# Forty edge buckets with halved sources, ranks summed on TensorE, and basis loads in 2 KB pieces

## The chip, the cores and the metric

The kernel runs on one core of one Trainium2 chip. The metric is the device time of one execution in microseconds; lower is better. Three executions of the kernel before took 2352.77 to 2354.81 us, median 2353.74.

## What is computed

```python
h = relu(layernorm(x))                       # x: 1250 nodes x 512
x = x + L0(h, edges, noise)                  # 4 blocks, each:
    # y = cond_layer_norm(x); q, k, v = y@wq, y@wk, y@wv, 4 heads of 128
    # scores only along 20000 edges src -> dst, softmax per src node, sum of v[dst]
    # x += attention @ wo;  x += relu(cond_layer_norm(x) @ m_w1) @ m_w2
h = relu(layernorm(x))
x = x + L1(h, edges, edge_type)              # 2 relational layers, each:
    # w[r]  = sum_b att[r, b] * basis[b]     # r in 0..1, b in 0..29, basis[b]: 512 x 512
    # gate  = sigmoid(x @ gate_w[r]);  msg[r] = (gate * x) @ w[r]
    # out   = sum over edges of type r of msg[r][dst] -> src,  + x @ root + bias
```

Edges may repeat, so both parts need, for each pair of nodes, how many edges of each type lie between them. The kernel makes this count matrix (1250 x 1250 x 2) on the chip and uses it as a bias of the scores (the logarithm of the count) and as the matrix of the relational sums. The combined relational weights w[r] take all 60 basis matrices, 1 MB each, through the chip.

## The kernel before, in words

Each of the five engines runs its own program in order, and semaphores tie them. The first 320 us hold three things at once.

**Edges to counts.** 20,000 edges lie as 128 x 157 in SBUF. DVE gives each edge a bucket (10 tiles of 125 destination nodes x 2 types, NB = 20), makes `mask[128, NB, EC]`, its running sum `cum` (L1641), and from the totals per bucket (two small matmuls, L824 and L825) the place of each edge in an order by bucket in which each bucket is padded to whole groups of 256 edges (L1648 to L1661). Then 10 sort batches (L1674 to L1682) build one-hot matrices on DVE, and PE (L841) moves source and destination numbers to their places. Then NG = 98 groups are counted: DVE builds `src_hot[128, 2, 1254]` (one-hot over all source nodes, L1705) and `dst_hot` (L1702), PE multiplies them into 3 banks of PSUM (6 matmuls of 418 columns, L859), ACT copies the result to 16-bit integers (`count_add`, L1328), and DVE adds it to the bucket's slice of `count` (L1716). There are two buffers of `src_hot` and of `count_add`; the addition of a group comes one iteration (two groups) behind its one-hots.

**Basis to relational weights.** SP loads the basis matrices in 80 loads of 768 KB (`load_bases`, L549), each 96 partitions (16 rows x 6 bases) x 8 KB, into a ring of 6 buffers; the ring frees a buffer when PE has used it. PE contracts each with the attention coefficients (`relation_loads`, 4 matmuls, L812). ACT stores the 16 results to HBM (L1278, L1280). PE takes its loads at fixed places of its program: 5 ahead of the sort, 2 or 3 behind each sort batch, and one behind every second count group (LOADS_FIRST, LOADS_SORT, LOADS_COUNT). Ahead of load 11 SP waits for ACT's `node_relu` (L1269) and stores x; ahead of load 65 it queues weights of the first block.

**Preparation** of the noise embedding (DVE L1619 to L1623, ACT L1284 to L1300, POOL L759), the normalisation of x (ACT), and constants on POOL (L701 to L721). POOL clears `count` (L773) when the places are known.

Then ten tiles of score biases are made and stored together with the counts (`adj`), and the four blocks run until about 1,950 us. Each relational layer then makes messages for ten tiles and sums them: for each tile t PE needs the counts of the tile, which SP loads (`load_adj`, L528) two tiles ahead into two buffers, and ACT turns to fp32 (`adj_hi`, L1536). Between the layers SP also loads the second layer's weights (`load_r`, L519, 8 transfers of 64 partitions for each type), queued ahead of the counts:

```python
sp.wait_ge(r_mm_ps, 3 * NT * (l + 1))
if l == 0:
    for n in range(3):
        load_r(1, n)
for t in range(NT):
    n = NT * l + t
    if n + 2 < 2 * NT:
        sp.wait_ge(r_adj_lo, n + 1)
        load_adj(n + 2)
```

## Time and profile before

| | us |
|---|---|
| median of three runs | 2353.74 (2352.77 to 2354.81) |
| profiled execution, its own time | 2352.55 |
| its span | 2350.8 |
| PE busy | 2202.4 (94%) |
| DVE busy | 1593.8 (68%) |
| ACT busy | 1119.3 (48%) |
| POOL busy | 546.2 (23%) |
| DMA moved | 189.56 MB |

The page's 40 slices are each 58.8 us long. The DMA row reads 9 8 9 9 9 6 in the first six, and 0 to 4 nearly everywhere behind; DVE's reads 9 9 8 9 9 8 there. PE's row is at 9 from the fifth slice on, with two exceptions in the slices 6 and 8, and at 2 and 8 in the first two. So the stretch up to about 320 us has other limits than the rest.

### The profile page before, as it was taken

Reading aid. Unit: us, or ns where it says so; the run is one execution under the profiler, and the core shown is the slowest. Engines: PE = TensorE matmul, PEld = TensorE weight load, DVE = VectorE, ACT = ScalarE, POOL = GpSimd, SP = SyncE. Lnnn points to the kernel's source line nnn. Section 1 sums busy time; section 2 is a strip of 40 time slices with the busy share of each in tenths; the row PEclk is TensorE's granted clock in tenths of the full one; section 3 lists DMA queues with packets and bytes.
Section 4 is the critical chain, followed back from the end, with each engine's and each line's share of the span. In section 5 each row is a group of like instructions: output and inputs, shape, how many; then the busy total and the mean of one; then the engine's idle time right before and its main releaser. Section 6 shows DMA issues by size and latency. Waiting matters only on the chain.

```text
span 2350.8 us, 36257 instructions
## 1 busy us (share of the span) xinstructions
PE 2202.4 (94%) x13797; PEld 1899.8 (81%) x13797; DVE 1593.8 (68%) x3322; ACT 1119.3 (48%) x1806; POOL 546.2 (23%) x401
## 2 busy tenths in 40 slices
PE   2889968999999999999999999999999999999998
PEld 1456647899988889988888998898899888877887
DVE  9989986478776458877646887763787774244233
ACT  5146652377743347763335775233677533222321
POOL 6000000066510026650003663000566200000000
PEclk9899978999999999999999999999999999999999
DMA  9899963111031011003102003111110421062034
GB/s 253 220 250 253 274 203 123 44 31 44 1 113 66 21 52 44 22 37 101 52 20 65 22 23 98 64 37 31 44 44 1 134 73 29 17 103 43 1 69 105
DMA packets 110945, 189.56 MB, mean 81 GB/s; under 512 B 57893, under 2 KB 58341, under 8 KB 103099
## 3 DMA queue, kind: packets, MB, share of 16 engines
q1 hardware_dynamic: 106776, 180.47, 28.9%
q10 hardware_dynamic: 4003, 6.79, 1.1%
q8 instruction: 114, 1.87, 0.3%
q14 instruction: 52, 0.43, 0.1%
HBM read 155.16 MB, written 32.07 MB: 80 GB/s over the span
## 4 chain that ended last, share of the span: by engine, by line
PE 75%; DVE 11%; issue 5%; ACT 5%; DMA 2%; DVEq 1%; SPq 1%; POOL 0%; ACTq 0%; POOLq 0%
PE PS L1043 10%; PE PS L1071 9%; PE PS L962 6%; PE PS L964 6%; PE PS L963 6%; PE PS L1057 6%; PE PS L948 5%; PE PS L952 4%; PE PS L949 4%; PE PS L1199 4%; PE PS L1209 4%; PE PS L859 3%; PE PS L812 2%; ACT prob L1433 1%; DMA basis_t<-in_L_gnn_basis_dram 1%
## 5 line engine op out<-in xcount | busy, mean ns | idle before, releaser
L793 POOL TENSOR_SCALAR prob<-prob,inv_den 125x1000 f32<-125x1000 f32 x160 | 444.5, 2778 | 0.0
L781 POOL TENSOR_TENSOR rstd<-var_eps,neg_half 125x2 f32<-125x2 f32 x45 | 35.4, 787 | 907.1 <-DVE var_eps L1596 907.1
L1433 ACT ACTIVATE prob<-prob,neg_max 125x1254 f32<-125x1254 f32 x160 | 215.5, 1347 | 56.9 <-DVE neg_max L1936 56.7
L1931 DVE CUSTOM_DVE_ANT_0 prob<-PS,sbias 125x1254 f32<-125x1254 f32 x160 | 233.0, 1456 | 11.0 <-issue 8.4
L1071 PE MATMUL PS<-pT_hi,v_hi 125*128 125x250 f32 x800 | 236.0, 295 | 0.0
L1950 DVE TENSOR_TENSOR pT_lo<-PS,pT_hi 125x1000 fp32r<-125x1000 f32 x160 | 191.1, 1194 | 51.2 <-ACT pT_hi L1450 51.2
L1071 PE MATMUL PS<-pT_lo,v_hi 125*128 125x250 f32 x800 | 224.1, 280 | 0.0
L1071 PE MATMUL PS<-pT_hi,v_lo 125*128 125x250 f32 x800 | 222.3, 278 | 0.0
L1057 PE MATMUL PS<-ident,prob 125*125 125x125 f32 x1600 | 201.7, 273 | 5.6 <-DVE pT_lo L1953 5.5
L1057 PEld LDWEIGHTS PS<-ident,prob 125*125 125x125 f32 x1600 | 196.1, 189 | 12.6 <-issue 7.6
L1448 ACT ACTIVATE pT_hi<-PS 125x1000 fp32r<-125x1000 f32 x160 | 161.8, 1011 | 82.7 <-PE PS L1057 82.7
L1328 ACT ACTIVATE count_add<-PS 125x1254 int16<-125x1254 f32 x98 | 118.9, 1215 | 72.3 <-PE PS L859 66.9
L1071 PEld LDWEIGHTS PS<-pT_lo,v_hi 125*128 125x128 f32 x800 | 151.9, 190 | 0.2
L1043 PE MATMUL PS<-k_hi,q_hi 128*125 128x418 f32 x480 | 125.0, 368 | 28.7 <-DVE row_max L1931 23.5
L1071 PEld LDWEIGHTS PS<-pT_hi,v_hi 125*128 125x128 f32 x800 | 151.6, 190 | 0.2
L1071 PEld LDWEIGHTS PS<-pT_hi,v_lo 125*128 125x128 f32 x800 | 151.3, 189 | 0.0
L859 PEld LDWEIGHTS PS<-src_hot,dst_hot 128*125 128x125 bf16 x588 | 100.7, 196 | 58.1 <-DVE src_hot L1705 54.4
L859 PE MATMUL PS<-src_hot,dst_hot 128*125 128x418 bf16 x588 | 132.4, 362 | 0.4 <-DVE src_hot L1705 0.4
L1510 ACT ACTIVATE hT_lo_raw<-PS,cols_all 128x250 f32<-128x250 f32 x80 | 37.5, 469 | 192.3 <-PE PS L952 192.3
L792 POOL TENSOR_TENSOR pool_slot<-pool_slot 1x1 f32<-1x1 f32 x160 | 29.3, 183 | 427.6 <-DVE inv_den L1944 427.6
L2102 DVE TENSOR_TENSOR adj_lo<-adj,adj_hi 125x2500 fp32r<-125x2500 int16 x20 | 55.2, 2762 | 99.2 <-PE PS L1209 87.1
L1043 PE MATMUL PS<-k_lo,q_hi 128*125 128x418 f32 x480 | 118.2, 355 | 0.0
(330 smaller groups left out, 5628.2 us busy)
## 6 DMA issues: line engine op xcount, KB each, us to landing
basis_t<-in_L_gnn_basis_dram SPq DMA_DIRECT2D x80, 768.0 KB, 12.5
sbias<-score_bias SPq DMA_DIRECT2D x40, 548.6 KB
adj<-adj SPq DMA_DIRECT2D x20, 546.9 KB
w_lo_raw<-in_L_gnn_m_w_dram SPq DMA_DIRECT2D x8, 1024.0 KB, 6.5
score_bias<-biases SPq DMA_DIRECT2D x10, 548.6 KB
adj<-count SPq DMA_DIRECT2D x10, 546.9 KB
xc<-x_lat SPq DMA_DIRECT2D x12, 448.0 KB
x_first<-x_lat SPq DMA_DIRECT2D x10, 448.0 KB
```

What stands on the lines that cost most here:

```text
L793: pool.tensor_scalar(prob[u % 3][:, 0:SPLIT], prob[u % 3][:, 0:SPLIT], inv_den[0:T, u % 4:u % 4 + 1], None, ALU.mult)\
L859: g = pe.matmul(PS[0:T, 3 * b + j, 0:SB], dst_hot[n // 2 % 2][:, 0:T, 2 * b + h], src_hot[b][:, h, SB * j:SB * (j + 1)], start=(h == 0), s ...
L962: pe.matmul(o, x_hi[:, k, n], w_hi[:, k, :], start=(k == 0), stop=False)
L963: pe.matmul(o, x_hi[:, k, n], w_lo[:, k, :], start=False, stop=False)
L964: g = pe.matmul(o, x_lo[:, k, n], w_hi[:, k, :], start=False, stop=(row3 is None and k == 3))
L1043: g = pe.matmul(PS[0:T, j, 0:SB], q_t[:, h, n], k_t[:, h, SB * j:SB * (j + 1)], start=(x == 0), stop=(x == 2))
L1057: g = pe.transpose(PS[0:T, 3 + k // 4, T * (k % 4):T * (k % 4 + 1)], prob[u % 3][:, T * k:T * (k + 1)], ident[0:T, 0:T])
L1071: g = pe.matmul(PS[:, 6 + s, 0:W], v_t[:, k, f], p_t[:, k, :], start=(k == 0 and x == 0), stop=(k == NT - 1 and x == 2))
L1433: act.activation(prob[u % 3][:], prob[u % 3][:], ACT.Exp, bias=neg_max[0:T, u % 4:u % 4 + 1], accum_out=den[0:T, u % 4:u % 4 + 1]).then_in ...
L1448: act.activation(pT_hi[i % 2][:, 0:8, n].rearrange("p (b c) t -> p b c t", b=2), PS[0:T, 3:5, 0:4 * T].rearrange("p b (c t) -> p b c t", c ...
L1931: v.tensor_tensor_reduce(prob[u % 3][:].rearrange("p (j s) -> p j s", j=3), PS[0:T, 0:3, 0:SB], sbias[p % 2][a][:].rearrange("p (j s) -> p ...
L1950: v.tensor_tensor(pT_lo[i % 2][:, 0:8, n].rearrange("p (b c) t -> p b c t", b=2), PS[0:T, 3:5, 0:4 * T].rearrange("p b (c t) -> p b c t", ...
```

## The change

1. NK = 40 buckets (NB = 20 before): type x destination tile x half of the sources. `count` is [125, 40, 628] in place of [125, 20, 1254], groups are NG = 118 in place of 98 (TC = 236 columns of places in place of 196), and a group has 4 matmuls of 314 columns in place of 6 of 418. `src_hot` and `count_add` have four buffers, and the addition comes two iterations behind.
2. Ranks: `mask` and `cum` are 16-bit and twice as long (6,280). The sum over buckets that DVE did in fp32 (L1655 to L1657) is split in a low part (DVE, 40 `tensor_scalar` and 4 products) and a high part (ACT, 40 activations), and PE adds the 40 slices of each with an identity matrix (80 matmuls of 157 columns). The table from groups to buckets is made by a transpose and one matmul. POOL makes a table `bucket_no[128, 40, 157]` ahead of `chunk_no`, `slot_no` and `group_no`, and DVE waits for all of them (14 constants).
3. Each basis load is four transfers of 96 partitions x 2 KB; the rows of a result follow. `load_r` therefore has 32 transfers of 16 partitions for each type in place of 8 of 64. PE takes 3 loads behind each sort batch and 3 behind every 8 count groups (79 ahead of the bias stage, as before).
4. In the relational layers `load_adj` comes ahead of `load_r`, and the three `load_r` are spread over the tiles 0 to 2.
5. `adj` is stored from the halves, in rows of 1,250 bytes (2,500 before).

```diff
-    NG = (EC * 128 + NB * (GE - 1)) // GE
+    NH = N // 2
+    HW = 628
+    HP = HW // 2
+    NK = 2 * NB
+    NG = (EC * 128 + NK * (GE - 1)) // GE
...
-        src_hot = [m(f"src_hot{i}", [128, 2, SW], bf16) for i in range(2)]
+        src_hot = [m(f"src_hot{i}", [128, 2, HW], bf16) for i in range(4)]
...
-        LOADS_SORT = [2 + b % 2 for b in range(SORT_BATCHES)]
-        LOADS_COUNT = [n % 2 for n in range(NG)]
+        LOADS_SORT = [3] * SORT_BATCHES
+        LOADS_COUNT = [3 * (n + 1) // 8 - 3 * n // 8 for n in range(NG)]
...
                     for k in range(D // GR):
-                        p0 = GR * (k % 2)
-                        sp.dma_start(wr_raw[n][p0:p0 + GR, k // 2, :],
-                                     rel_w[l, k, :, :].rearrange("(j r i) d -> r i j d", j=4, r=R)[n]).then_inc(rel_in[n], 16)
+                        for j in range(4):
+                            p0 = GR * (k % 2) + GROUP_I * j
+                            at = GROUP_I * (R * j + n)
+                            sp.dma_start(wr_raw[n][p0:p0 + GROUP_I, k // 2, :], rel_w[l, k, at:at + GROUP_I, :]).then_inc(rel_in[n], 16)
...
-                sp.dma_start(basis_t[n % RING][:], rows.rearrange("b (i j) d -> i b (j d)", j=4)).then_inc(basis_in[n % RING], 16)
+                for j in range(4):
+                    sp.dma_start(basis_t[n % RING][:, j, :], rows[:, GROUP_I * j:GROUP_I * (j + 1), :].rearrange("b i d -> i b d"))\
+                        .then_inc(basis_in[n % RING], 16)
...
                 sp.wait_ge(r_mm_ps, 3 * NT * (l + 1))
-                if l == 0:
-                    for n in range(3):
-                        load_r(1, n)
                 for t in range(NT):
                     n = NT * l + t
                     if n + 2 < 2 * NT:
                         sp.wait_ge(r_adj_lo, n + 1)
                         load_adj(n + 2)
+                    if n < 3:
+                        load_r(1, n)
...
+            pool.iota(bucket_no[:], [[1, NK], [0, EC]], base=0, channel_multiplier=0,
+                      allow_small_or_imprecise_dtypes=True).then_inc(consts, 1)
...
+            pe.wait_ge(rank_step, BASES)
+            for part in range(4):
+                pe.wait_ge(rank_step, LOW_RANKS + part)
+                for k in range(NK // 4 * part, NK // 4 * (part + 1)):
+                    pe.matmul(PS[:, 5, 0:EC], ident16[:], cum[:, k, :], start=(k == 0), stop=(k == NK - 1))
+            for part in range(4):
+                pe.wait_ge(rank_hi_done, part + 1)
+                for k in range(NK // 4 * part, NK // 4 * (part + 1)):
+                    g = pe.matmul(PS[:, 4, 0:EC], ident16[:], rank_hi[:, k, :], start=(k == 0), stop=(k == NK - 1))
+            g.then_inc(rank_ps, 1)
...
-            link(v.tensor_tensor(rank[:], cum[:], base[:].unsqueeze(2).to_broadcast([128, NB, EC]), ALU.add))
-            link(v.tensor_tensor(rank[:], rank[:], mask[:], ALU.mult))
-            link(v.tensor_reduce(pos[:], rank[:].rearrange("p k c -> p c k"), AX.X, ALU.add))
...
+            link(v.scalar_tensor_tensor(base_lo[:], base_hi[:], -128.0, base[:], ALU.mult, ALU.add))
+            for part in range(4):
+                ks = slice(NK // 4 * part, NK // 4 * (part + 1))
+                for k in range(ks.start, ks.stop):
+                    last = v.tensor_scalar(cum[:, k, :], cum[:, k, :], base_lo[:, k:k + 1], None, ALU.add)
+                link(last)
+                v.tensor_tensor(cum[:, ks, :], cum[:, ks, :], mask[:, ks, :], ALU.mult).then_inc(rank_step, 1)
+            v.wait_ge(rank_ps, RANK_PS)
```

On DVE, the ranks, from the running sum to the first one-hot of the sort. Before:

```order
L1641 SCALAR_TENSOR_TENSOR cum<-mask 128x3140 [waits chain]
...
L1655 TENSOR_TENSOR rank<-cum,base 128x3140 [waits chain]
L1656 TENSOR_TENSOR rank<-rank,mask 128x3140 [waits chain]
L1657 TENSOR_REDUCE pos<-rank 128x157 [waits chain]
L1658 TENSOR_SCALAR pos_c<-pos 128x157 [waits chain]
```

In the change (the middle two parts of four are like the first):

```order
L1680 SCALAR_TENSOR_TENSOR cum<-mask 128x6280 [waits chain]
...
L1704 TENSOR_SCALAR cum<-cum,base_lo 128x157 [waits chain]
L1704 TENSOR_SCALAR cum<-cum,base_lo 128x157 x9
L1706 TENSOR_TENSOR cum<-cum,mask 128x1570 [waits chain]
...
L1708 TENSOR_SCALAR pos<-PS 128x157 [waits rank_ps]
```

DVE now waits for PE between the last product and the places.

On SP, from the first relational layer's messages to its sums. Before:

```order
L519 DMA wk_lo_raw<-rel_w 64x1x512 [waits r_mm_ps]
L519 DMA wk_lo_raw<-rel_w 64x1x512 x7
L519 DMA wv_lo_raw<-rel_w 64x1x512 x8
L515 DMA wq_lo_raw<-in_L_gnn_root_dram 128x4x512
L528 DMA adj_136<-adj 112x20x125 [waits r_adj_lo]
L528 DMA adj_136<-adj 13x20x125
```

In the change:

```order
L542 DMA adj_136<-adj 112x20x125 [waits r_adj_lo,r_mm_ps]
L542 DMA adj_136<-adj 13x20x125
L534 DMA wk_lo_raw<-rel_w 16x512 x32
L542 DMA adj_137<-adj 112x20x125 [waits r_adj_lo]
L542 DMA adj_137<-adj 13x20x125
L534 DMA wv_lo_raw<-rel_w 16x512 x32
L542 DMA adj_136<-adj 112x20x125 [waits r_adj_lo]
```

The counts of tile 2 stand first, and 32 transfers stand between two loads of counts.

## Rows read from the trace of the kernel before

**Rows 1.** Windows of four stretches (busy us per engine, PEclk, DMA share, GB/s).

```profile
core 0: us, PE busy (x) PEld busy (x) DVE busy (x) ACT busy (x) POOL busy (x), PEclk, DMA share, GB/s
140.00:235.00 95.00, 94.83 (x530) 58.28 (x526) 94.39 (x184) 66.64 (x60) 0.00 (x0) 1.00 1.01 253
300.00:310.00 10.00, 10.00 (x57) 6.00 (x57) 10.00 (x21) 7.78 (x7) 0.00 (x0) 1.00 0.12 41
651.00:654.00 3.00, 2.86 (x25) 2.66 (x24) 1.51 (x2) 3.00 (x6) 2.92 (x2) 1.00 1.04 399
673.00:678.00 5.00, 5.00 (x28) 4.10 (x27) 3.96 (x10) 1.99 (x3) 0.70 (x1) 1.00 1.08 235
```

**Rows 2.** DMA issues by line (KB each, median us to landing).

```profile
basis_t<-in_L_gnn_basis_dram SPq DMA_DIRECT2D x80, 768.0 KB, 12.5
```

**Rows 3.** Chain that ended last, 30 to 135 us (start, us, what).

```profile
115.92 17.18 DMA basis_t<-in_L_gnn_basis_dram
```

**Rows 4.** Groups of instructions, 135 to 312 us (busy, mean ns | idle before).

```profile
L859 PE MATMUL PS<-src_hot,dst_hot 128*125 128x418 bf16 x588 | 132.4, 362 | 0.4 <-DVE src_hot L1705 0.4
L1328 ACT ACTIVATE count_add<-PS 125x1254 int16<-125x1254 f32 x97 | 117.7, 1215 | 72.2 <-PE PS L859 66.9
L1705 DVE TENSOR_SCALAR src_hot<-node_no,slot_src 128x1254 bf16<-128x1254 f16 x192 | 95.3, 535 | 0.0
L1716 DVE TENSOR_TENSOR count<-count,count_add 125x1254 int16 x96 | 76.4, 796 | 0.5 <-issue 0.3 <-ACT count_add L1328 0.2
L1702 DVE TENSOR_TENSOR dst_hot<-slot_no,slot_dst 128x512 bf16<-128x512 f16 x48 | 19.6, 409 | 5.3 <-PE PS L859 5.2
```

**Rows 5.** Timeline of all engines, 311 to 357 us (start, us, line, what).

```profile
313.66 0.81 DVE L1716 TENSOR_TENSOR count<-count,count_add 125x1254 int16 x1 [0.52 <-ACT count_add L1328]
```

**Rows 6.** Timeline of DVE, 0 to 62 us.

```profile
14.57 3.43 DVE L1638 TENSOR_TENSOR mask<-bucket,bucket_id 128x3140 bf16<-128x3140 f32 x1
...
18.03 6.70 DVE L1641 TENSOR_TENSOR_SCAN cum<-mask 128x3140 f32<-128x3140 bf16 x1
...
27.09 3.43 DVE L1655 TENSOR_TENSOR rank<-cum,base 128x3140 f32<-128x3140 f32 x1
...
34.02 5.83 DVE L1657 TENSOR_REDUCE pos<-rank 128x157 f32<-128x3140 f32 x1
...
41.17 2.95 DVE L1674 TENSOR_SCALAR chunk_hot<-chunk_no,pos_c 128x196 f16<-128x196 f16 x16
...
44.05 1.21 DVE L1678 TENSOR_TENSOR place_hot<-edge,slot_no 128x2048 f16<-128x2048 f16 x1
```

**Rows 7.** Timeline of POOL, 0 to 100 us.

```profile
2.53 2.47 POOL L717 IOTA slot_no<- 128x2048 f16 x1
...
15.06 10.51 POOL L730 TENSOR_TENSOR att_z<-att_rows,row_of 96x80 f32<-96x80 f32 x4 [7.46 <-DMA att_rows<-in_L_gnn_att_dram]
...
47.88 10.57 POOL L773 MEMSET count<- 125x12540 f32 x1
```

**Rows 8.** Line L1674, 49 to 62 us (ns min/median/max).

```profile
L1674 DVE TENSOR_SCALAR chunk_hot<-chunk_no,pos_c x16: 253/258/8440, 50.1 to 60.8; 128x196 f16<-128x196 f16 x16
```

**Rows 9.** Timeline of PE, 0 to 140 us.

```profile
32.90 6.30 PE L812 MATMUL PS<-basis_t,att_z 96*32 96x512 f32 x40
```

**Rows 10.** Costliest groups of the page.

```profile
L1510 ACT ACTIVATE hT_lo_raw<-PS,cols_all 128x250 f32<-128x250 f32 x80 | 37.5, 469 | 192.3 <-PE PS L952 192.3
```

**Rows 11.** Timelines of SP, ACT and PE, 2,040 to 2,280 us.

```profile
2050.49 5.74 SPq L519 DMA_DIRECT2D wk_lo_raw<-rel_w  x8
...
2056.26 5.05 SPq L519 DMA_DIRECT2D wv_lo_raw<-rel_w  x8
...
2276.15 0.33 SPq L686 DMA_DIRECT2D xres<-x_lat  x1
...
2072.12 2.29 ACT L1536 ACTIVATE adj_hi<-adj 125x2500 fp32r<-125x2500 int16 x1 [21.03 <-DMA adj<-adj]
...
2074.46 5.93 PE L1199 MATMUL PS<-msg_hi,adj_hi 125*125 125x512 f32 x18 [5.35 <-ACT adj_hi L1536]
```

More of the change, by code:

```diff
@@ L1289, in _ @@
             act.activation(cols_all[:, 2:4, :], cols[:, 2:4, :], ACT.Copy).then_inc(cols_out, 1)
+            act.wait_ge(rank_step, BASES)
+            for k in range(NK):
+                h = act.activation(rank_hi[:, k, :], mask[:, k, :], ACT.Copy, scale=base_hi[:, k:k + 1])
+                if (k + 1) % (NK // 4) == 0:
+                    h.then_inc(rank_hi_done, 1)
             act.wait_ge(z1_ps, 1)
```

196 lines of the change are left out of this document (110 added, 86 removed).

## The prediction

> **What bounds the kernel now.** I read the page's 40 slices first: DMA is busy in nine tenths only at the beginning, PE in nine tenths only behind it. So I cut the first 320 us into windows. From 140 to 235 us the DMA share is 1.01 at 253 GB/s, and DVE is busy in 94.39 of 95 us; by 300 to 310 us the share is down to 0.12 while counting goes on [rows 1]. Two limits lie side by side there: the 80 basis transfers of 768 KB, 786 KB in thousands of bytes [rows 2], which at 253 GB/s take 3.1 us each, and the vector work of 98 groups. The chain of waits shows what ends last in the sort: it runs over two long waits for a basis load, the second of them 17.18 us [rows 3]. In the counting the groups of instructions tell the rest: DVE was idle 5.3 us ahead of `dst_hot` and hardly elsewhere, while ACT waited 66.9 us for PE's groups [rows 4]. So the sort is held by the basis and the counting by DVE; the last addition ends at 313.66 + 0.81 = 314.5 us [rows 5]. All that follows waits for it, and PE is then the bound to the end. What the change does ahead of 314.5 us therefore counts in full, once.
>
> **The change, part by part.**
>
> *Start of the sort.* The order on DVE is unchanged up to the bucket, but DVE now waits for 14 constants, among them `bucket_no`. POOL's `slot_no` took 2.47 us for 2,048 elements [rows 7], 1.21 ns each, so 6,280 take 7.6 us more ahead of the mask. The mask is two times 3,140 elements, but 16-bit on its input too: at the 1.21 us of `place_hot` for 2,048 [rows 6] it takes 3.7 against 3.43. The scan took 6.70 us for 3,140 [rows 6] with 16-bit input already, so 13.4: +6.7. The ranks cost DVE two products of 3.43 and a sum of 5.83, 12.7 us in all [rows 6]; now 40 short operations, at the 0.18 us of a `chunk_hot` (2.95 / 16, [rows 6]) 7.2 us, and four products of 1,570 elements, by `place_hot` 0.93 each: 10.9 us, -1.8. Behind them stands the wait on PE, which is new. PE is to finish five basis loads first; they began at 32.90 and took 6.30 us [rows 9], and they wait for `att_z`, which POOL begins at 15.06 and makes for 10.51 us [rows 7]. With the constants 7.6 us later and a longer DVE lock (POOL's 10.51 us already hold gaps for DVE) they end at 48 to 52. ACT's 40 activations of 157 columns, at 469 ns for 250 fp32 columns [rows 10], are 12 us at about 0.3 each, parallel to DVE; PE's last 40 sums follow part by part. That gives about +7 us. Sum: 7.6 + 6.7 - 1.8 + 7 + 2.5 for the short steps around them = 22 us: the sort starts at about 63.5 instead of 41.2. The bounds: +14 if PE and ACT keep up wholly, +30 if POOL and DVE lock each other out more. One such lock is in the trace: an operation of 258 ns took 8440 ns [rows 8], until POOL's clearing of `count` (47.88 + 10.57, [rows 7]) was over; it stays.
>
> *Vector work of sort and counting.* In the sort DVE makes 16 `chunk_hot` of 236 columns instead of 196 (about 0.19 us) and three products of 1.21 to 1.5 per batch: 6.6 to 7 us, ten batches and the lock, 76 us. Alone it would end at 63.5 + 76 + 8 for the two first batches and PE's tail, near 148. In the counting a group cost 2 x 535 + 796 + 409 / 2 = 2,070 ns by [rows 4], but (314.5 - 133.1) / 98 = 1.85 us by the clock, since neighbouring operations overlap (133.1 is where the counting begins, 115.92 + 17.18 [rows 3]). Half as wide, `src_hot` is about 0.3 us and the addition 0.41; `dst_hot` stays at 0.205 per group. 0.59 + 0.41 + 0.205 = 1.2, by the same overlap 1.15 to 1.17. 118 groups: 138 us in place of 181. ACT's copy, 1,215 ns for 1,254 columns [rows 4], comes to 0.65 to 0.76 for 628; PE's four matmuls of 314 to 0.66, and three loads per eight groups add 0.4. Neither reaches 1.17. So DVE alone would be ready at 148 + 138 + 2 = 288 us: **26 us earlier**.
>
> *The basis stream.* It must keep up, and this is the unknown. Its limit is a rate. Load 12 waits for ACT's `node_relu` and the stores of x, which move with the start by 21 us, to about 85 us. From there 68 loads follow: in the kernel before 64 + 68 x (3.11 + 0.2) + 10 = 299 us (0.2 for the stores of results, 10 for the weights of the first block and gaps), which fits the quiet DMA at 300 us [rows 1]. After: 85 + 68 x (786 / rate + 0.2) + 10. What is the rate of 96 partitions x 2 KB? No transfer of the trace has that shape. Weights of 128 partitions x 2 KB came at 399 GB/s, x in 112 partitions x 2 KB at 235 [rows 1], the basis in 96 x 8 KB at 253. Of the two slow shapes one is no whole number of quarters of the partitions, the other has long pieces; the new one has neither fault, and in pieces it is nearest to the 399. But it reaches three quarters of the partitions, so three quarters of 399, 299 GB/s, is what I hold for the ceiling. The bounds are 235 and 299, beyond them 399 only if partitions don't matter. I take 290, a little under the ceiling, because the stream also pays SP's time: a piece of `load_r` took SP 5.05 / 8 to 5.74 / 8 us, a row of x in 125 pieces of 2 KB 0.33 [rows 11], so four pieces cost 1.3 to 2.9 us beside the 2.7 us of the transfer. Then the last load ahead of the bias is there at 85 + 68 x 2.91 + 10 = 293, DVE's path gives 288, and with both near the end the counting ends at **294 us, -20.5**.
>
> [...]
>
> *Relational layers.* SP queued 17 transfers of `load_r` ahead of the counts of tile 2, the first at 2050.49; ACT, idle for 21.03 us, had the counts only at 2072.12, and PE stood 5.35 us [rows 11]. Now the counts go first, and this wait goes: -5.4. What is late next: 32 transfers of 16 partitions stand between two counts. At 0.63 us each as above they take SP 20 us, at the 0.33 of `xres` [rows 11] 11 us; PE needs some 10 us for a tile (two halves, the first of which took 5.93 us for most of its matmuls, [rows 11]). At 0.33 each count is queued about when PE begins the tile two ahead of its own, and nothing stalls. At 0.63 the counts of tile 4 are queued at 2050 + 2 x 21.5 = 2093, used at 2100 instead of 2088, and PE stalls 12 us there: +12 - 5.4 = +7. Sixteen pieces are fewer than either row has, so I take 0.33 to 0.4 and put back 2 us: net **-3.4**, with -5.4 and +7 as bounds.
>
> *Small edits.* `adj` in rows of 1,250 bytes: twice the pieces for 5.5 MB, beside the bias stage, which waits for other things; +1.5 (0 to 3). `load_r` of the last blocks in four times the pieces, hidden by PE's work of many us; +0.5. The transpose for `group_tile` is on PE in the sort: nothing, the cover is DVE's batch.
>
> **Sum**: -20.5 - 3.4 + 1.5 + 0.5 = -21.9 us. The profiled execution took 2352.55, 1.2 under the median, so 2330.6 for it, and 2332 against the median of 2353.74.
>
> **Rivals.**
>
> *The rate stays at 253.* A partition still gets the same 8 KB, and the early loads of the x tiles show that 2 KB alone doesn't make a transfer fast (235). Then 85 + 68 x 3.31 + 10 = 320, DMA ends the counting at about 319: +4.5 - 1.4, time **2357**. For it: the bytes per partition and the partitions are the same. [...] The point from which the change pays is (314.5 - 85 - 10) / 68 - 0.2 = 3.03 us a load, 260 GB/s.
>
> *In between*, 262 to 282 GB/s: the counting ends between 311 and 298, time **2335 to 2350**; also where SP's issue of 2.9 us a load becomes the limit, or where the 32 transfers between the counts of the relational layer stall PE.
>
> *Small transfers are slower: 235 GB/s, the rate of the 112 x 2 KB row.* 85 + 68 x 3.54 + 10 = 336, in the sort and counting some 333: +18.5 - 1.4, **2371**, slower than before. For it: that row is the only 2-KB one with part of the partitions. Against it: those transfers had small ones of 13 partitions between them.
>
> *A fully quick stream* (over 320): DVE's 288, time 2326; with `bucket_no` and PE's wait cheaper than I put them, 2320.
>
> **Numbers.** My forecast, 290 to 320 and more, has 0.40 (2320 to 2334); in between 0.18; the rate stays 0.26; lower 0.16. A measurement of this kernel tells 0.2%, 4.7 us, from no change. Faster: 0.40 + 0.16 of the second = 0.56. The same: 0.02 + 0.16 of the third = 0.18. Slower: 0.10 of the third, where the sort starts later than I put it, + 0.16 = 0.26. The range from 2319 to 2366 leaves out 0.05 below and half of the last rival above.
>
> **What would show it.** `bucket_no` on POOL at 7.6 us, the scan at 13.4, the first `chunk_hot` at about 63 (of a range of 55 to 71). In windows of the stretch from 100 to 280 us: GB/s near 290 and a DMA share under 1 at times. The groups: `src_hot` near 300 ns, the addition at 410, 1.17 us a group. The last addition near 294. In the first relational layer no wait of PE on `adj_hi` at tile 2. I am wrong if DMA is at a share of 1.0 with 253 GB/s or less and DVE waits for PE in the counting, if the sort begins after 71 us, or if a new wait of over 5 us stands at the tiles 3 to 5.

## The result and the profile after

| | before | after |
|---|---|---|
| median, us | 2353.26 (2350.09 to 2354.81, 4 runs) | 2384.11 (2383.26 to 2385.77, 4 runs) |
| ratio | | 1.0139, interval 1.0125 to 1.0153 |
| span of the profiled execution | 2350.8 | 2381.5 |

The change makes the kernel 31 us slower; 2332 with a range from 2319 to 2366 was forecast. I laid both traces side by side and read off when each stage begins. `csum` is DVE's first operation behind the last addition, `bias_mod` its first one of block 0 behind the score biases.

| stage begins, us | before | after | behind by | lost in the stage before it |
|---|---|---|---|---|
| sort (first `chunk_hot`) | 41.2 | 57.2 | 16.0 | 16.0 |
| counting (first matmul) | 135.0 | 150.3 | 15.3 | -0.7 |
| score biases (first `csum`) | 314.6 | 323.6 | 9.0 | **-6.3** |
| block 0 (`bias_mod`) | 355.2 | 370.5 | 15.3 | **+6.3** |
| x of the relational part (`xr`) | 1904.1 | 1925.2 | 21.1 | **+5.8** |
| end | 2350.8 | 2381.5 | 30.7 | **+9.7** |

So there are four places. The first three rows are the part on which the forecast stood: there the counting was to win 43 us and won 6. The column before is one execution, and two of its stages move. In the runs below that leave them as they are, `csum` began up to 3.5 us earlier (f and m), and the stage from `xr` to the end took 449 to 453 us instead of 446.7 (b, c, l and m). So the change lost 9 to 12.5 us ahead of `csum`, and 3 to 10 us in the last stage.

**The basis stream** did what was hoped, and more. Windows of the changed kernel (columns as in [rows 1]):

```profile
core 0: us, PE busy (x) PEld busy (x) DVE busy (x) ACT busy (x) POOL busy (x), PEclk, DMA share, GB/s
120.00:180.00 60.00, 53.72 (x374) 30.24 (x372) 46.37 (x119) 22.42 (x35) 2.84 (x1) 0.94 1.06 310
200.00:240.00 40.00, 31.45 (x190) 17.17 (x189) 34.40 (x96) 20.21 (x30) 0.00 (x0) 1.00 0.67 211
340.00:370.00 30.00, 13.44 (x60) 11.93 (x60) 20.82 (x18) 9.22 (x13) 0.00 (x0) 0.61 1.05 295
```

310 GB/s over 60 us, where the kernel before had 253 [rows 1]; from 200 us on the share is 0.67: the transfers wait for PE (SP 13.4 us in the 40, PE for no load), no longer the other way round. The last window is in the bias stage, and comes up below.

**Start of the sort.** Timeline of POOL, then of DVE, in the changed kernel:

```profile
3.88 6.01 POOL L775 IOTA bucket_no<- 128x6280 f16 x1
```

```profile
19.64 3.45 DVE L1678 TENSOR_TENSOR mask<-bucket,bucket_no 128x6280 f16<-128x6280 f16 x1
23.12 13.24 DVE L1680 TENSOR_TENSOR_SCAN cum<-mask 128x6280 f16<-128x6280 f16 x1
...
55.07 0.32 DVE L1708 TENSOR_SCALAR pos<-PS 128x157 f32<-128x157 f32 x1 [4.30 <-PE PS L863]
...
57.19 3.14 DVE L1728 TENSOR_SCALAR chunk_hot<-chunk_no,pos_c 128x236 f16<-128x236 f16 x16
...
62.63 3.85 DVE L1736 TENSOR_TENSOR dst_place<-place_hot,edge 128x2048 f16<-128x2048 f16 x1
66.40 12.34 DVE L1728 TENSOR_SCALAR chunk_hot<-chunk_no,pos_c 128x236 f16<-128x236 f16 x16
```

`bucket_no` took 6.01 us and the scan 13.24, twice that of [rows 6]; DVE waited 4.30 us for PE's sums. The last two rows show DVE held by POOL in the first two batches, as in [rows 8]: POOL's `z * z` ran from 61.97 for 3.42 us and its clearing of `count` from 65.34 for 10.58.

**The counting.** Groups of instructions of the changed kernel from 152 to 322 us (busy, mean ns | idle before), the counterparts of [rows 4]:

```profile
L892 PE MATMUL PS<-src_hot,dst_hot 128*125 128x314 bf16 x464 | 94.1, 325 | 34.5 <-DVE src_hot L1757 33.8 <-ACT count_add L1366 0.7
L1366 ACT ACTIVATE count_add<-PS 125x628 int16<-125x628 f32 x117 | 81.1, 694 | 83.7 <-PE PS L892 78.9 <-DVE count L1768 4.7
L1757 DVE TENSOR_SCALAR src_hot<-node_no,slot_src 128x628 bf16<-128x628 f16 x228 | 76.4, 378 | 0.0
...
L1768 DVE TENSOR_TENSOR count<-count,count_add 125x628 int16 x116 | 56.4, 486 | 23.9 <-issue 17.3 <-ACT count_add L1366 2.6 <-DVE count L1768 0.9
```

PE now stands 34.5 us, ACT 83.7; DVE stands 23.9 us ahead of its additions, 17.3 of it with the releaser "issue". That word means that nothing the profile shows kept it. Two groups in DVE's timeline show the pattern:

```profile
205.25 0.42 DVE L1754 TENSOR_TENSOR dst_hot<-slot_no,slot_dst 128x512 bf16<-128x512 f16 x1
205.58 0.67 DVE L1757 TENSOR_SCALAR src_hot<-node_no,slot_src 128x628 bf16<-128x628 f16 x2
206.37 0.49 DVE L1768 TENSOR_TENSOR count<-count,count_add 125x628 int16 x1
206.77 0.67 DVE L1757 TENSOR_SCALAR src_hot<-node_no,slot_src 128x628 bf16<-128x628 f16 x2
207.62 0.49 DVE L1768 TENSOR_TENSOR count<-count,count_add 125x628 int16 x1 [0.18 <-issue]
208.15 0.43 DVE L1754 TENSOR_TENSOR dst_hot<-slot_no,slot_dst 128x512 bf16<-128x512 f16 x1
```

From 205.25 to 208.15 a pair of groups takes 2.90 us, 1.45 a group (and (323.6 - 150.3) / 118 = 1.47 over all). The operations of one group need no more than 0.59 + 0.39 + 0.17 = 1.15 from start to start if they follow closely. The rest is between them: ahead of an addition 0.2 us, and 0.53 from the last addition to `dst_hot` where 0.40 would do. The run without reads, below, takes just these 1.15 us.

What the engine's sequencer does in these gaps is not counted as busy, but the view of one source line lists it. First the line that reads the table in the changed kernel, then the one in the kernel before (ns min/median/max):

```profile
L1763 DVEq FUSED_REGOPS  x230: 53/190/216, 152.3 to 322.6; - x115
L1763 DVEq TENSOR_LOAD <-group_tile x118: 298/304/1117, 151.7 to 322.2; - x118
```

```profile
L1711 DVEq TENSOR_LOAD <-group_tile x98: 299/305/1105, 137.4 to 312.4; - x98
```

Each group has one `TENSOR_LOAD` of 0.30 us, one register operation of 0.19 behind it and short steps around them. They are as long before as after; what changed is the work beside which they run.

**Last block and relational layer.** SP's timeline, PE's, and from the table of waits DVE's wait for x (engine, line, what ended it: us in total, times, longest):

```profile
1867.74 15.86 SPq L534 DMA_DIRECT2D wk_lo_raw<-rel_w  x32
1883.64 2.62 SPq L524 DMA_DIRECT2D xc<-x_lat  x6
...
2076.86 16.44 SPq L534 DMA_DIRECT2D wk_lo_raw<-rel_w  x32
2093.34 2.37 SPq L542 DMA_DIRECT2D adj<-adj  x2
...
2111.99 2.41 SPq L542 DMA_DIRECT2D adj<-adj  x2
```

```profile
2102.76 6.35 PE L1232 MATMUL PS<-msg_hi,adj_hi 125*125 125x512 f32 x20 [3.23 <-ACT adj_hi L1574]
...
2121.60 7.10 PE L1232 MATMUL PS<-msg_hi,adj_hi 125*125 125x512 f32 x20 [7.85 <-ACT adj_hi L1574]
```

```profile
DVE xc L2035 <- DMA xc<-x_lat: 3.0, 1, 3.0
```

32 transfers of 16 partitions occupy SP for about 16 us, 0.5 us each, where 8 of 64 partitions took 5 [rows 11]. In the last block the loads of x stand behind them, in the relational layer the counts of tiles 3 and 4: PE stands 3.23 and 7.85 us, in place of the 5.35 on tile 2 [rows 11], which is gone. And a stall costs more than its length: the 20 matmuls behind it took 6.35 and 7.10 us instead of 4.8. Behind the second stall the granted clock was 0.50 from 2,121 to 2,126 us; the mean from 2,100 to 2,120 is 0.82. The 5.35 us of before [rows 11] had the same sequel, 6.39 us for the 20 matmuls.

### The profile page after: what moved, and what is told of

Its sections match the earlier page's. It is cut to its first block, busy times and chain, and to the rows that moved or that the text cites. A ratio compares the mean times of both kernels' runs of the same rounds, so it can differ in the third digit from the quotient of the medians.

```text
span 2381.5 us, 36959 instructions
## 1 busy us (share of the span) xinstructions
PE 2183.4 (92%) x13763; PEld 1884.0 (79%) x13763; DVE 1577.8 (66%) x3441; ACT 1095.4 (46%) x1866; POOL 551.7 (23%) x403
## 4 chain that ended last, share of the span: by engine, by line
PE 71%; DVE 11%; issue 6%; ACT 5%; SPq 3%; DVEq 2%; DMA 2%; POOL 0%; ACTq 0%
PE PS L1076 10%; PE PS L1104 9%; PE PS L995 6%; PE PS L997 6%; PE PS L996 6%; PE PS L1090 6%; PE PS L981 5%; PE PS L985 4%; PE PS L982 4%; PE PS L1232 3%; PE PS L1242 3%; SPq L534 2%; ACT prob L1471 1%; DVE src_hot L1757 1%; PE PS L916 1%
## 5 line engine op out<-in xcount | busy, mean ns | idle before, releaser
L892 PEld LDWEIGHTS PS<-src_hot,dst_hot 128*125 128x125 bf16 x472 | 68.0, 197 | 88.6 <-DVE src_hot L1757 85.0
L809 POOL TENSOR_TENSOR pool_slot<-pool_slot 1x1 f32<-1x1 f32 x160 | 29.5, 185 | 427.6 <-DVE inv_den L1996 427.6
L892 PE MATMUL PS<-src_hot,dst_hot 128*125 128x314 bf16 x472 | 95.5, 324 | 34.5 <-DVE src_hot L1757 33.8
L1366 ACT ACTIVATE count_add<-PS 125x628 int16<-125x628 f32 x118 | 81.7, 694 | 92.4 <-PE PS L892 87.6
```

Source lines behind the costliest of these rows:

```text
L892: g = pe.matmul(PS[0:T, 2 * b + j, 0:HP], dst_hot[n // 2 % 2][:, 0:T, 2 * b + h], src_hot[n % 4][:, h, HP * j:HP * (j + 1)], start=(h == 0 ...
```

## The experiments

All times are medians, each beside runs of the kernel before on the same chip; the ratio to it is given with its 95% interval. Subtractions of two variants mostly go across chips, on which the kernel before has medians from 2350.3 to 2353.3, so differences of under 3 us say nothing. One reading has to be made with care: in the profiles of the runs f and m, whose work ahead of it takes as long as that of before, `csum` began at 311.2 and 311.0 instead of 314.6, so a difference of 3 us ahead of it proves nothing.

### One read of the table less in each group (run d)

```diff
-                k = v.value_load(group_tile[0:1, bass.ds(2 * it + b, 1)], min_val=0, max_val=NK - 1)
-                tile = count[:, bass.ds(k, 1), :].rearrange("p a s -> p (a s)")
+                tile = count[:, 20 * b, :]
```

> The changed kernel, with the addition always going to bucket 0 or 20 in place of the one read from the table of groups (so the counts are not the edges'). Theory: in short groups DVE's sequencer is the limit, with the reading of the table's number the costliest step; DVE is idle 0.18 to 0.26 us ahead of each addition (issue). Without it a group takes 1.25 us instead of 1.46: 25 us less, 2359. Rival: the group is bound by DVE's operations themselves (0.67 + 0.49 + 0.21 us) and the wait on PE and ACT; then 1.4 us or more and at least 2377.

Measured: 2344.38 us, ratio 0.9978 (0.9966 to 0.9989), 40 us under the changed kernel. The timeline of DVE:

```profile
202.23 0.41 DVE L1754 TENSOR_TENSOR dst_hot<-slot_no,slot_dst 128x512 bf16<-128x512 f16 x1
202.57 0.66 DVE L1757 TENSOR_SCALAR src_hot<-node_no,slot_src 128x628 bf16<-128x628 f16 x2
203.16 0.47 DVE L1767 TENSOR_TENSOR count<-count,count_add 125x628 int16<-125x628 int16 x1
203.55 0.66 DVE L1757 TENSOR_SCALAR src_hot<-node_no,slot_src 128x628 bf16<-128x628 f16 x2
204.14 0.47 DVE L1767 TENSOR_TENSOR count<-count,count_add 125x628 int16<-125x628 int16 x1
204.53 0.41 DVE L1754 TENSOR_TENSOR dst_hot<-slot_no,slot_dst 128x512 bf16<-128x512 f16 x1
```

A pair takes 2.30 us, 1.15 a group, without a gap; `csum` begins at 287.6. The operations are as long as ever (0.66 and 0.47). So the operations had been priced well in the forecast, and the read was missing from it. Of the 40 us, 36.5 lie in the counting (136.8 us from its first matmul to `csum` instead of 173.3), 0.31 us a group, where I had expected 0.21; 4.4 lie in the bias stage. The edit also makes the address of the addition a fixed one, so this run alone doesn't part the read from what follows it; the next but one does.

### The same reads, placed ahead (run i)

```diff
+                    ks = [read_group(it - 2, b) for b in range(2)]
                     for b in range(2):
                         one_hot(it, b, turn)
-                        add_group(it - 2, b, turn)
+                        add_group(it - 2, b, turn, k=ks[b])
```

> The changed kernel, with the two numbers of a pair of groups read from the table ahead of the pair's one-hots instead of each just ahead of its addition (as many reads as before). Theory A: a read costs DVE's sequencer its own time (0.31 us a group, by the run without reads), wherever it stands; then a group still takes 1.46 us and the time is 2384 within 4. Theory B: what costs is the latency between the read and the addition that uses it; then it hides behind the one-hots, a group takes 1.2 us and the time is near 2355.

Measured: 2410.42 us, ratio 1.0253 (1.0238 to 1.0267), worse than either theory had it. DVE's timeline:

```profile
204.18 0.67 DVE L1757 TENSOR_SCALAR src_hot<-node_no,slot_src 128x628 bf16<-128x628 f16 x2
204.77 0.48 DVE L1772 TENSOR_TENSOR count<-count,count_add 125x628 int16 x1
206.43 0.42 DVE L1754 TENSOR_TENSOR dst_hot<-slot_no,slot_dst 128x512 bf16<-128x512 f16 x1 [1.18 <-PE PS L892]
```

Nothing stands ahead of an addition any more, but 1.18 to 1.43 us stand ahead of `dst_hot`, once in a pair. The profile writes this wait to PE (the semaphore that came last in the row's wait), but PE's last group ahead of it was over at 204.91 + 0.81 = 205.72, 0.71 us before `dst_hot` starts. What lies there till the end is the two reads. PE's row, and the line of the reads on DVE's sequencer from 204.8 to 206.3 us (ns min/median/max, first and last start):

```profile
204.91 0.81 PE L892 MATMUL PS<-src_hot,dst_hot 128*125 128x314 bf16 x4 [0.17 <-DVE src_hot L1757]
```

```profile
L1762 DVEq FUSED_REGOPS  x3: 57/190/190, 205.2 to 205.9; - x3
L1762 DVEq TENSOR_LOAD <-group_tile x2: 299/300/301, 204.9 to 205.6; - x2
L1762 DVEq SEQ_ASSERT  x2: 23/23/23, 205.5 to 206.2; - x2
```

The first `TENSOR_LOAD` starts at 204.9, 0.1 us behind the start of the addition, the second at 205.6, and the last step of the reads at 206.2, 0.2 us ahead of `dst_hot`. PE then stood 1.78 us for the next `src_hot`, until 207.50. The pair takes 3.57 us, 1.27 more than without reads. Theory B is out: it isn't latency that could be hidden by reading early. Theory A is out in its second half, "wherever it stands": the earlier place lost what cover the reads had.

### Each read twice (run j)

```diff
-                k = v.value_load(group_tile[0:1, bass.ds(2 * it + b, 1)], min_val=0, max_val=NK - 1)
+                for _ in range(2):
+                    k = v.value_load(group_tile[0:1, bass.ds(2 * it + b, 1)], min_val=0, max_val=NK - 1)
```

> The changed kernel with each number read twice from the table, one read behind the other. Theory A (sequencer time, nothing hides it): another 0.31 us or a little less for each of 118 groups, 2384 + 30 to 37 = 2414 to 2421. If the first read's cost is one of waiting for the operations ahead of it, the second is nearly free and the time is under 2395.

Measured: 2460.76 us (2 executions), ratio 1.0466 (1.0448 to 1.0484); over the changed kernel 76.65 us, and 76.65 / 118 = **0.65 us a read**. That is twice what I expected. All of it is in the counting, which takes 249.9 us instead of 173.3. Only reads were added here, so it is the read. The first read of a group costs 0.31 (the run without reads), the second 0.65. DVE's timeline, and the line of the reads on its sequencer from 203.7 to 205.2 us, show one group:

```profile
203.73 0.67 DVE L1757 TENSOR_SCALAR src_hot<-node_no,slot_src 128x628 bf16<-128x628 f16 x2
205.28 0.48 DVE L1769 TENSOR_TENSOR count<-count,count_add 125x628 int16 x1 [0.89 <-issue]
```

```profile
L1764 DVEq FUSED_REGOPS  x3: 75/190/190, 203.7 to 204.7; - x3
L1764 DVEq TENSOR_LOAD <-group_tile x2: 304/304/305, 203.8 to 204.4; - x2
L1764 DVEq SEQ_ASSERT  x2: 23/23/23, 204.3 to 205.0; - x2
```

The first read starts at 203.8 and runs while DVE works on the `src_hot` pair, until 204.40; the second starts at 204.4 and finds nothing left to run beside, and DVE stands 0.89 us ahead of the addition. The reads ahead fit as well: 1.27 us more in a pair are 0.64 for each of its two reads. The `TENSOR_LOAD` has only 0.30 of the 0.65 us.

### No reads in the kernel before (run m)

```diff
-                k = v.value_load(group_tile[0:1, bass.ds(2 * it + b, 1)], min_val=0, max_val=NB - 1)
-                tile = count[:, bass.ds(k, 1), :].rearrange("p a s -> p (a s)")
+                tile = count[:, 10 * b, :]
```

> The kernel before, with the addition always going to bucket 0 or 10, so without reading the table (the counts are not the edges'). Theory: a read takes DVE's sequencer 0.65 us (76.6 us for 118 doubled reads) and lies, in the kernel before, wholly behind the pair of src_hot of 0.99 us that DVE is still working on; the group stays at 1.80 us and the time at 2351 within 4. Rival: the read was exposed in the kernel before as well, and what the change lost is something else; then 98 x 0.34, 33 us less, 2318.

Measured: 2349.43 us, ratio 0.9999 (0.9989 to 1.0009): nothing. A pair still takes 3.60 us:

```profile
199.98 0.42 DVE L1702 TENSOR_TENSOR dst_hot<-slot_no,slot_dst 128x512 bf16<-128x512 f16 x1
200.32 1.01 DVE L1705 TENSOR_SCALAR src_hot<-node_no,slot_src 128x1254 bf16<-128x1254 f16 x2
201.23 0.81 DVE L1715 TENSOR_TENSOR count<-count,count_add 125x1254 int16<-125x1254 int16 x1
```

The next `dst_hot` starts at 203.59. So the same read that costs the changed kernel 36.5 us costs the kernel before nothing that shows (some 2 us either way by the interval): its two `src_hot` take 0.99 us together and cover it. Halving the operations' length took the cover away. This settles the main term.

### Basis pieces of 2 KB and of 4 KB, alone, in the kernel before (runs b and c)

```diff
-                sp.dma_start(basis_t[n % RING][:], rows.rearrange("b (i j) d -> i b (j d)", j=4)).then_inc(basis_in[n % RING], 16)
+                for j in range(4):
+                    sp.dma_start(basis_t[n % RING][:, j, :], rows.rearrange("b (i j) d -> i j b d", j=4)[:, j, :, :])\
+                        .then_inc(basis_in[n % RING], 16)
...
```

(That is run b; run c has two transfers, and PE's wait counts to 64 or 32.)

> The kernel before, with only the basis loads changed: four transfers of 96 partitions x 2 KB, each partition's 8 KB cut in four, same data at same places. Theory: the length of the piece a partition gets sets the rate; the stream goes from 253 to 305 to 320 GB/s, the two waits of the sort (16 + 17 us) shrink to under 8 together, the counting begins at about 110 and, bound by DVE at 1.85 us a group, ends at about 291: time 2330. Rival: the rate in the changed kernel comes from its own order of rows or its pauses, not from the pieces; then the rate stays at 253 and the time at 2353.

> The kernel before, basis loads in two transfers of 96 partitions x 4 KB. Theory of the piece's length: the rate lies between 253 and 315, near 285, the time near 2340. Theory that it is the number of transfers queued at a time or any piece below 8 KB: full 310 GB/s, the time as with 2 KB. No effect of the piece: 2353.

Measured: 2347.70 us, ratio 0.9989 (0.9977 to 1.0000), and 2351.37, ratio 0.9994 (0.9980 to 1.0008). Windows of the first, then of the second (columns as in [rows 1]):

```profile
100.00:120.00 20.00, 16.82 (x155) 9.69 (x153) 19.90 (x51) 5.79 (x10) 3.74 (x1) 1.00 1.05 314
...
260.00:280.00 20.00, 20.00 (x116) 12.19 (x114) 20.00 (x40) 14.29 (x13) 0.00 (x0) 1.00 1.06 305
```

```profile
140.00:160.00 20.00, 20.00 (x115) 12.15 (x114) 19.70 (x39) 13.95 (x13) 0.00 (x0) 1.00 1.03 285
```

The rate follows the length of the piece: 253 GB/s at 8 KB, 285 at 4 KB, 305 to 314 at 2 KB (310 in the changed kernel), with the same partitions and the same bytes for each. The number and the size of the transfers change along with the piece (one of 768 KB, two, four of 192 KB), so which of them sets the rate isn't told apart. SP's timeline of the first run from 100 to 140 us, where the rate was 301 to 314 GB/s:

```profile
99.83 40.52 SPq L550 DMA_DIRECT2D basis_t<-in_L_gnn_basis_dram  x59
```

That is 0.69 us for a piece, 2.7 us for a load, with 2.7 us of waits for PE in the 40.52; at 308 GB/s, the mean there, a load takes 2.6 us.

The time doesn't follow: the counting still began at 130.1, where in the runs f and m, with the slow stream, it began at 131.4 and 132.0. What held the sort then stands in the chain of waits of the first run:

```profile
41.25 17.25 DVE chunk_hot L1676 x16
```

DVE, held by POOL (its product `z * z` from 42.77 for 5.17 us and its clearing of `count` from 47.90 for 10.54), had its first `chunk_hot` ready only after 17.25 us, and then nine more batches of 6.4 us before it; from there to 120.8 us the chain has nothing but DVE in it. The waits of 16 and 17 us for the basis in the chain of before [rows 3] had lain over the same stretch of DVE's work. The chain shows the one that ended last, and I read it as the only one.

### Clearing `count` on ACT, alone, in the kernel before (run l)

```diff
             node_relu()
+            act.wait_ge(pos_ready, 1)
+            act.activation(count[:].bitcast(fp32), tiny[0:T, :].unsqueeze(2).to_broadcast([T, NB, SW // 2]), ACT.Copy,
+                           scale=0.0).then_inc(count_zero, 1)
...
-            pool.wait_ge(pos_ready, 1)
-            pool.wait_ge(z1_ps, 1)
-            pool.memset(count[:].bitcast(fp32), 0.0).then_inc(count_zero, 1)
```

> The kernel before, with the clearing of count on ACT alone. With the 2 KB pieces alone the sort ended only 3 to 4 us earlier, since DVE (held by POOL's clearing) was hardly ahead of the stream. Theory: two limits lie level in the sort of before, so freeing DVE alone gives as little as freeing the stream alone: 0 to -4 us, 2349 to 2353. Rival: DVE's time is the real limit and the waits for the basis only its echo; then -10, near 2342.

Measured: 2341.63 us, ratio 0.9964 (0.9952 to 0.9976), 8 to 9 us faster; my theory of two level limits falls, the rival holds. ACT's and DVE's timelines:

```profile
50.95 10.71 ACT L1301 ACTIVATE count<-tiny 125x12540 f32<-125x12540 f32 x1
```

```profile
45.22 3.73 DVE L1681 TENSOR_TENSOR src_place<-place_hot,edge 128x2048 f16<-128x2048 f16 x1
...
50.01 2.97 DVE L1674 TENSOR_SCALAR chunk_hot<-chunk_no,pos_c 128x196 f16<-128x196 f16 x16
```

The second batch's `chunk_hot` take 2.97 us where they took 11.00 with the 8,440-ns operation of [rows 8] among them. The remaining 3.73 for `src_place` (1.22 elsewhere) lies beside POOL's `z * z` (43.04 to 47.86).

PE still waits for the basis in this run's sort (us in total, times, longest), while its counting begins at 124.3:

```profile
PE PS L809 <- DMA basis_t<-in_L_gnn_basis_dram: 9.2, 4, 2.7
```

### Weights of the relational layers: 8 transfers again (runs a and e)

Twice, the first time with the new order of rows kept:

```diff
-                        for j in range(4):
-                            p0 = GR * (k % 2) + GROUP_I * j
-                            at = GROUP_I * (R * j + n)
-                            sp.dma_start(wr_raw[n][p0:p0 + GROUP_I, k // 2, :], rel_w[l, k, at:at + GROUP_I, :]).then_inc(rel_in[n], 16)
+                        p0 = GR * (k % 2)
+                        sp.dma_start(wr_raw[n][p0:p0 + GR, k // 2, :],
+                                     rel_w[l, k, :, :].rearrange("(j r i) d -> r j i d", j=4, r=R)[n]).then_inc(rel_in[n], 16)
...
```

> The changed kernel, with each type's relational weights read in 8 transfers of 64 partitions again instead of 32 of 16 (the same rows, the same places). Theory: each small transfer costs SP about 0.5 us whatever its size, so 32 hold SP for 16 us; that delays the loads of x in the last block (5.8 us of PE) and the counts of the tiles 3 and 4 in the relational layer (3.2 + 7.9 us of PE). Then both go: 2384 - 5.8 - 11.1, about 2367, and more where PE's wait on tile 2 of before (5.4) is gone as well. Rival: SP is not the limit, the DMA queues are shared with stores or the counts come late for their 250-byte rows; then the time stays at 2384 within 3 us.

Measured: 2373.66 us, ratio 1.0097 (1.0079 to 1.0114): 10.5 us better where 17 were expected. SP needed only 4.8 us for the 8 transfers, but DVE still waited for x in the last block and PE in the relational layer:

```profile
DVE xc L2034 <- DMA xc<-x_lat: 3.2, 1, 3.2
...
PE PS L1231 <- ACT adj_hi L1573: 5.0, 1, 5.0
```

The packets of these loads moved at 100 GB/s, in the kernel before at some 200. A window in which, by SP's timeline, only these loads are under way, in this run and then in the kernel before (columns as in [rows 1]):

```profile
2080.00:2083.00 3.00, 3.00 (x15) 2.37 (x14) 2.91 (x4) 1.36 (x1) 0.00 (x0) 1.00 0.26 102
```

```profile
2053.00:2056.00 3.00, 3.00 (x15) 2.38 (x14) 0.26 (x1) 0.00 (x0) 0.00 (x0) 1.00 0.75 214
```

A share of 0.26 is what four of the 16 DMA engines would give. In this form the source's outermost dimension has 4 entries, in the kernel before 16. So the second time with the old order of rows and `"(j r i) d -> r i j d"`, and the 2 KB pieces cut as in the run above:

> The changed kernel with 2 KB pieces that keep the old order of rows (partition i holds rows 4i to 4i+3), so that each type's weights are read in 8 transfers of 64 partitions exactly as before. With the 8 transfers of the run before, whose outermost dimension was 4, the pieces moved at about 100 GB/s and x still came late; with 16 as the outermost dimension they moved at 200. Theory: the outermost dimension of a transfer decides over how many of the 16 DMA engines it is spread. Then the last block loses nothing (-5.8 us) and the relational layer has neither its stalls of 11.1 us nor the old one of 5.4: 2384 - 5.8 - 11 or slightly more, 2366 to 2368. Rival: it is the number of transfers alone, and the time stays at the 2373.7 of the 8-transfer run.

Measured: 2363.86 us, ratio 1.0050 (1.0032 to 1.0067), 20 us under the changed kernel, and in neither place a wait is left. That the outermost dimension decides over how many engines a transfer is spread stays my reading. The two windows above show this much: 16 entries went with a share of 0.75, 4 with one of 0.26, at 214 and 102 GB/s, and the order of the rows differed as well.

### Counts first, alone, in the kernel before (run f)

```diff
-                if l == 0:
-                    for n in range(3):
-                        load_r(1, n)
                 for t in range(NT):
                     n = NT * l + t
                     if n + 2 < 2 * NT:
                         sp.wait_ge(r_adj_lo, n + 1)
                         load_adj(n + 2)
+                    if n < 3:
+                        load_r(1, n)
```

> The kernel before, with only the order on SP in the first relational layer changed: counts first, one group of relational weights behind each of the tiles 0 to 2. Theory: PE's 5.35 us on tile 2 go and nothing comes in their place, 2353 - 5.4, about 2348. Rival: the counts of tile 3 or 4 become late by what tile 2 gains; then within 1.5 us of before.

Measured: 2343.77 us, ratio 0.9967 (0.9951 to 0.9983). PE has no wait on `adj_hi` in the first relational layer. The gain is 8 us with an interval from 4 to 11.5. With 8 transfers of 5 us between two counts the reordering is worth its 5.35 us of waiting and the 1.6 us that the matmuls behind the wait lost; the rest is inside the interval. In the changed kernel the same reordering traded a wait of 5.35 us for 11.1, because 16 us of SP stood between the counts.

### Counts stored in pieces of 5 KB (run g)

```diff
-                                 count[r0:r1, 4 * t:4 * t + 4, 0:NH]).then_inc(adj_stored, 16)
+                                 count[r0:r1, 4 * t:4 * t + 4, :]).then_inc(adj_stored, 16)
```

(with `adj` widened to rows of 628 and its loads moved to fit.)

> The changed kernel, with the counts stored for the relational layers in a padded layout, so that a partition's two buckets x two halves are one piece of 5,024 bytes instead of four of 1,250. Theory: the bias stage is a matter of the DMA rate (share 1.05 at 296 GB/s, before up to 374), and the short pieces cost its extra 6.3 us: about 2378. Rival: the stage is longer because the stores begin behind something else; then 2384.

Measured: 2378.39 us, ratio 1.0112 (1.0093 to 1.0131), 5.7 under the changed kernel; the stage from `csum` to `bias_mod` took 40.9 us (before 40.7, changed 46.9). In the changed kernel, the chain had stood on stores there, twice for 11 us:

```profile
342.17 11.09 DMA score_bias<-biases
```

The DMA share is 1.05 at 295 GB/s there (window from 340 to 370 us, above). One thing speaks for caution: in other runs with pieces of 1,250 bytes the stage took 42.6 us (run d), 44.7 (a), 44.9 (i), 45.6 (j) and 47.5 (e), so the loss isn't the same wherever the stage falls. The 5.7 us are measured, the 6.3 of the table are one execution of a stage that moves by 5.

### Combinations (runs k, h and n)

The changed kernel with the rows of the run e, 5 KB pieces of counts, and the clearing on ACT:

> The changed kernel with the rows and weights of the run e, the counts stored in 5,024-byte pieces as in the run g, and the clearing of count on ACT. The first two are independent: 2363.9 - 5.7 = 2358. Theory: DVE's 10.5 us in the sort come on top, 2348. Rival: the sort of the changed kernel is held by its three loads per batch (SP needs 4 x 0.63 us for each, 7.6 us a batch against 6.6 us of DVE), so most of the 10 us go to the wait for the basis: 2354 to 2358.

Measured: 2352.54 us, ratio 1.0003 (0.9994 to 1.0012). 11.3 under the run e, of which 5.7 are the pieces by run g; so the clearing brought 5 to 6 of its 8 to 9 us. The rest went to the basis, it seems, as the rival had it: PE waits 9.4 us for it in the sort, 3.0 in the changed kernel.

```profile
PE PS L827 <- DMA basis_t<-in_L_gnn_basis_dram: 9.4, 7, 1.9
```

The kernel before with 2 KB pieces, counts first and the clearing on ACT:

> The kernel before with three edits: basis in 2 KB pieces (old order of rows), counts first in the relational layer, and the clearing of count done by ACT behind node_relu instead of by POOL. [...] The sort ends 10 us earlier: 2353 - 3 (2 KB) - 5.4 - 10, about 2335. Rival: what holds DVE is POOL's product z * z and the first batch itself, and the time is 2344.

Measured: **2330.46 us, ratio 0.9907 (0.9891 to 0.9923)**, faster than both kernels by 21 and 54 us. Its `csum` begins at 301.2. PE's waits in its sort:

```profile
PE PS L839 <- DVE dst_place L1683: 17.0, 9, 9.1
...
PE PS L810 <- DMA basis_t<-in_L_gnn_basis_dram: 1.0, 1, 1.0
```

By the same view PE waited 10.4 us for the basis in the kernel before and 9.2 with the clearing alone (run l); with the 2 KB pieces it is 1.0. But the time hardly follows: the counting begins 4.9 us earlier than in run l, `csum` 3.0. Alone the pieces gave 3 us at most, the clearing 9 and the counts 8, in sum 20, and together they give 21. So they add up, and that the pieces are worth more once DVE is freed is not shown. Nor does a run show the 10 us put on the clearing above: alone it gave 8 to 9 (run l).

The same with the counts stored in pieces of 5,016 bytes instead of 2,500:

> The run h with the counts stored in pieces of 5,016 bytes (a partition's two buckets as one) instead of 2,500. In the changed kernel pieces of 5,024 instead of 1,250 gave 5.7 us. Theory: the bias stage of before is held by the DMA rate too, with half as many pieces to lose: -2 to -4, 2327 to 2329. Rival: at 2,500 bytes the pieces are long enough, 2330.5.

Measured: 2329.94 us, ratio 0.9920 (0.9906 to 0.9934), the same: from 2,500 bytes on a longer piece brings nothing that shows there.

## Why the prediction was wrong

Step by step, against 2383.3 for the profiled execution (2330.6 forecast for it, 52.7 too little):

| term | forecast | measured | off by |
|---|---|---|---|
| end of the counting | 294 | 323.5 | +29.5 |
| storing the counts | +1.5 | +6.3 | +4.8 |
| `load_r` in the last block | +0.5 | +5.8 | +5.3 |
| relational layer | -3.4 | +9.7 | +13.1 |

- **Start of the sort**: 57.2, forecast 63.5. `bucket_no` took 6.0 instead of 7.6 us, PE's part 4.3 of DVE's time instead of 7. Within the bounds. But the counting began at 150.3, where 148 was forecast: the sort took 93 us instead of 84.5, and the 6 us were gone.
- **The basis stream**: right in direction, short in size. 310 GB/s; I had taken 290 and called 299 a ceiling, which three quarters of 399 is not; that whole quarters of the partitions matter no run shows, since all loaded 96. Bounds and rivals were nearly all about this term, and the rate turned out harmless: both rivals with a slow stream are refuted, and the time is slower all the same.
- **"So the sort is held by the basis"**: wrong for the kernel before, and shown so by two runs. The quick stream alone gave 3 us or nothing, DVE alone 9. In the changed kernel the sort takes 93 us with a stream a quarter faster, as before. There PE has 30 loads to take in it instead of 25, and from 82 us on the chain of waits leaves DVE: it runs over PE's work, and at the end over SP's queueing of basis pieces (0.60 us each, from 135.7) and their landing at 149.2. So the forecast's "DVE alone" of 84.5 us for the sort was not what bound it.
- **The failed step: "0.59 + 0.41 + 0.205 = 1.2, by the same overlap 1.15 to 1.17. 118 groups: 138 us in place of 181."** The sum holds DVE's operations and leaves out what its sequencer does between them. Without the reads it is met exactly (1.15), the overlap of neighbouring operations included. With them a group takes 1.46 to 1.47, 118 of them 173 us. In the kernel before the read had a cover, a pair of `src_hot` of 0.99 us, and the sum took for granted that it has one behind 0.67 us too. That is 0.30 x 118 = 35 us more than forecast. The end of the counting is off by 29.5 only, because the forecast had put 294 where DVE's own path gave 288. The read is the largest term, and enough for the loss by itself: without it the kernel is 0.2% faster than before (run d), with the other places mended, the clearing on ACT and the read left in (run k) it is level.
- **`load_r` in the last block, "hidden by PE's work of many us; +0.5"**: I looked for what waits for the weights and not for what is queued behind them. 0.5 us x 32 instead of 0.6 x 8 is 11 us more of SP, and the six loads of x stand behind. With the old rows and 8 transfers (run e) the stage is back at 1548.3 us, before 1548.9.
- **Relational layer**: the mechanism was priced, with the wrong value. I took 0.33 to 0.4 us for a transfer of 16 partitions, from the row of `xres`, and had +7 as the upper bound with 0.63; measured was 0.5, with +9.7. That transfer is in the upper half of the two rows, and the counts' own 2.4 us of SP and their landing came on top. PE's waits grew by 11.1 - 5.35 = 5.7 us, and the matmuls behind them, which the sum leaves out, lost 3.8 us instead of 1.6. The rest of the 9.7 is inside the spread of the stage. Of the signs of being wrong that the prediction names, this one came: a new wait of 7.85 us, on the counts of tile 4.
- **Storing the counts**: the piece's length was named and put at 1.5, with 3 as a bound; it cost 5.7 by run g (6.3 in the table). "Beside the bias stage, which waits for other things" was wrong: in the changed kernel the stage has a DMA share near 1, and its chain stands on stores.

The rival on the other side that I had put on a slow stream named the wrong mechanism. The right one was "DVE's sequencer becomes the bound in short groups", for which the trace of before had a hint that I didn't follow: it has a `TENSOR_LOAD` of 0.30 us for every addition, 98 in all (the row of L1711 above).

## What to carry to other kernels

- Before operations on an engine are halved, count what its sequencer does between two of them: register reads, waits, branches. Here a read of a table of 0.65 us cost nothing that shows behind 0.99 us of work (run m) and 0.31 us behind 0.67 (run d); where nothing was left to run beside, it cost all of it (run j).
- In a stretch where an engine is busy 9 tenths and the chain stands on a transfer, don't name one of them as the limit: take each away alone. Here one gave 3 us at most, the other 9.
- A transfer costs SP nearly as much when it is small: 0.5 us for 32 KB, 0.6 to 0.7 for 128 KB here. Cutting a load in four raised the rate of a stream that had SP to itself (253 GB/s before, 310 after), but with urgent loads queued behind it PE stood 11.1 us; so look at what is queued behind before you cut.
